# A four-layer graph network: the mixing products of three layers as 64x64 products in four quarters of the array

## What is computed

```python
# gnn, twice: W_left, W_right, W_lin per sublayer
u = u_left * adj_tri + u_left * diag_mask + u_right * swapaxes(adj_tri, 1, 2)
delta_exp_u = exp(u) * adj
attention = delta_exp_u / (sum(delta_exp_u, axis=2, keepdims=True) + 1e-10)
ctx = matmul(attention, h @ W_lin.T + b_lin)          # 64x64 times 64x384, per graph
h = relu(layer_norm(ctx) * ln_a + ln_b)

# gcn, twice: Wl, Ws, Wr per sublayer
attn = delta / (sum(delta, -1, keepdims=True) + 1e-10)   # delta = softmax(h h.T / temper) * adj
ctx = einsum(attn * upper, hl) + diag(attn)[..., None] * hs + einsum(attn * lower, hr)
h = relu(layer_norm(ctx) * g + beta)
```

## Time and profile before

| | |
|---|---|
| median of 3 runs | 3187.76 us (3184.48 to 3189.42) |
| the profiled execution: its time, its span | 3182.71 us, 3180.9 us |
| PE, DVE, ACT, POOL busy share of the span | 91%, 63%, 32%, 31% |
| granted TensorE clock, mean over the span | 0.968 of 2.4 GHz |
| steady period of a group: gnn first, gnn second | 25.99 us, 26.34 us |
| steady period of a group: gcn first, gcn second | 29.30 us, 29.13 us |

### The profile page before, as it was taken

How to read it: one execution, slowest core, us unless ns; L and a number is a source line. 1 busy time by engine, 2 the same in 40 slices (tenths; PEclk the granted TensorE clock), 3 DMA queues, 4 the chain that set the end, 5 groups by cost and what they waited for, 6 DMA issues and landing times.

```text
span 3180.9 us, 70089 instructions
## 1 busy us (share of the span) xinstructions
PE 2889.1 (91%) x25280; PEld 2445.8 (77%) x25280; DVE 2001.0 (63%) x4582; ACT 1014.4 (32%) x1921; POOL 974.3 (31%) x908
## 2 busy tenths in 40 slices
PE   6999979999959999997999997999996689899998
PEld 5888868888847777776888886888885577777776
DVE  4444434555556676666777775776776477777776
ACT  2333322333324444443222222122121333333432
POOL 1222213444433333332101110243334143334333
PEclk9999989999979999998999998999998899999999
DMA  3222242333311112112122114222222011111110
GB/s 97 70 69 69 59 129 77 99 99 99 96 61 45 45 45 66 45 52 88 44 64 64 54 43 126 64 75 94 94 75 89 31 45 45 45 35 33 45 35 33
DMA packets 197219, 210.27 MB, mean 66 GB/s; under 512 B 72736, under 2 KB 197024, under 8 KB 197024
## 3 DMA queue, kind: packets, MB, share of 16 engines
q1 hardware_dynamic: 197024, 207.33, 21.1%
HBM read 131.80 MB, written 75.50 MB: 65 GB/s over the span
## 4 chain that ended last, share of the span: by engine, by line
PE 52%; DVE 11%; issue 6%; ACT 1%; POOL 1%; DMA 1%; DVEq 0%; POOLq 0%; ACTq 0%
PE psum L1010 18%; PE psum L822 14%; PE psum L826 4%; DVE v_x L1419 3%; PE psum L1041 3%; PE psum L1040 3%; PE psum L851 2%; PE psum L840 2%; PE psum L895 2%; DVE room L1447 2%; PE psum L1022 2%; PE psum L872 1%; DVE room L1463 1%; DVE room L1377 1%; PE psum L863 1%
## 5 line engine op out<-in xcount | busy, mean ns | idle before, releaser
L1010 PE MATMUL psum<-fast 128*128 128x384 f32 x3456 | 647.8, 341 | 20.4 <-issue 8.1
L1010 PEld LDWEIGHTS psum<-fast 128*128 128x128 f32 x3456 | 596.2, 188 | 49.3 <-DVE room L1377 15.5
L1377 DVE TENSOR_TENSOR room<-psum,rows 128x384 f32<-128x384 f32 x512 | 283.9, 555 | 312.5 <-PE psum L1010 168.4
L822 PE MATMUL psum<-fast 128*128 128x512 f32 x1728 | 464.7, 416 | 3.8 <-DVE fast L1407 3.0
L694 PE MATMUL psum<-fast 128*128 128x512 f32 x1728 | 417.5, 398 | 16.2 <-DVE fast L1364 16.2
L694 PEld LDWEIGHTS psum<-fast 128*128 128x128 f32 x1728 | 327.0, 190 | 90.5 <-issue 16.9
L822 PEld LDWEIGHTS psum<-fast 128*128 128x128 f32 x1728 | 324.7, 196 | 75.5 <-issue 4.9
L540 POOL TENSOR_TENSOR room<-room 128x768 f32<-128x768 f32 x128 | 188.7, 1474 | 482.2 <-DVE room L1453 296.5
L826 PE MATMUL psum<-fast 128*128 128x384 f32 x1152 | 235.3, 348 | 42.8 <-DVE v_x L1419 30.1
L1211 ACT ACTIVATE room<-psum 128x512 f32<-128x512 f32 x192 | 114.6, 597 | 426.6 <-PE psum L694 426.6
L610 POOL TENSOR_TENSOR room<-room,halfs 128x4 f32<-128x4 f32 x32 | 33.3, 1042 | 704.8 <-DVE room L1699 704.8
(11 more groups left out here) (107 smaller groups left out, 4480.1 us busy)
## 6 DMA issues: line engine op xcount, KB each, us to landing
x_ring<-x_mid SPq DMA_DIRECT2D x64, 768.0 KB, 4.6
x_mid<-x_ring SPq DMA_DIRECT2D x48, 768.0 KB, 4.1
x_ring<-x_in SPq DMA_DIRECT2D x32, 768.0 KB, 4.6
z_mid<-x_ring SPq DMA_DIRECT2D x32, 768.0 KB, 4.1
z_sb<-z_mid SPq DMA_DIRECT2D x32, 768.0 KB, 5.9
adjc<-adj SPq DMA_DIRECT2D x96, 128.0 KB, 4.1
out<-x_ring SPq DMA_DIRECT2D x16, 768.0 KB, 4.1
w_raw<-w_all SPq DMA_DIRECT2D x19, 576.0 KB, 4.3
```

The lines of the kernel that those rows point to most:

```text
L822: mm = nc.tensor.matmul(dst, wpart[m][:, c, oc * P:(oc + 1) * P], hpart[G.par][:, c], start=(k == 0), stop=(k == 3 * C - 1))
L1010: mm = nc.tensor.matmul(dst[:, 0:H], hpart[G.par][:, c, t * P:(t + 1) * P], wpart[m][:, c, :], start=(k == 0), stop=(k == 3 * C - 1))
L1377: done(nc.vector.tensor_tensor(dst, src, rows[:, m], ALU.add), "evac_n")
```

## The change

- In gnn and gcn a mixing product is 64x64: one graph's matrix in one quarter of the array, 64 rows by 64 columns. The row half of a quarter is set by the partitions of the two operands, its column half by the partitions of the output. Two row halves that work at the same time write to different banks.
- gnn: `mix(g, pair)` issues four products, for a and b in (0, 1), with operands in row half b and output in column half a. For that the graphs of a group are taken in another order in stages 1 and 2: the turning writes its columns permuted, and the adjacency is read from two arrays that the host has permuted (`adj_q`, `adj_t`). `d_x` with its zeros becomes `d_k`, filled by one POOL operation of 128 partitions.
- gcn: the projection for the lower triangles is made with its rows shifted by one graph (`first_row`), so a graph's `hr` stands in the other partition half than its `hl`. The last tile wraps round to graph 0, for which ACT copies 64 columns behind the activations (`ninth_graph`, two operations for each group). Lower and upper products of different tiles then fill the four quarters: sixteen products in four rounds of four. Rounds 3 and 4 accumulate on rounds 1 and 2 and wait for them (`fs`). `d_x2` is half as large and filled by three DVE operations instead of four.
- Waits: the first gnn pair waits for `evac_n` 1 and the second for 3, before it was one for each tile; the gcn mixing waits at its start for `evac_n` 11, before for 8 to 11 in turn. DVE's `context` waits for a pair of tiles, and `gather` takes tiles 0, 2, 1, 3, the first two released after round 3 and the others after round 4.
- The memsets of the zeros are gone.

```diff
 # gnn, POOL
-                        for a in (0, 1):
-                            r = slice(a * S, (a + 1) * S)
-                            done(nc.gpsimd.tensor_tensor(d_x[r, :, r], et[r], biasc[r, g.par], ALU.mult), "dT")
+                        done(nc.gpsimd.tensor_tensor(d_k, et, biasc[:, g.par], ALU.mult), "dT")
 # gnn, TensorE
+                            turned = bank_of(g + 1, H_SLOT[c]).rearrange("p (i a b k) -> p i b a k", i=2, a=2, b=2)
                             for t in range(T):
-                                mm = nc.tensor.transpose(bank_of(g + 1, H_SLOT[c])[:, t * P:(t + 1) * P],
-                                                         z_sb[:, t, c * P:(c + 1) * P], ident)
+                                mm = nc.tensor.transpose(turned[:, t // 2, t % 2], z_sb[:, t, c * P:(c + 1) * P], ident)
...
-                    def mix(g, t):
-                        if t == 0:
-                            after(pe, "dT", g, 1)
-                        after(pe, "evac_n", g, t)
-                        after(pe, "z1", g + -1, t)
-                        done(nc.tensor.matmul(psum[:, 4 + t, 0:H + 1], d_x[:, t], lin[:, g.par, t], start=True, stop=True),
-                             "cx")
+                    def mix(g, pair):
+                        if pair == 0:
+                            after(pe, "dT", g, 0)
+                        after(pe, "evac_n", g, 2 * pair + 1)
+                        after(pe, "z1", g + -1, 2 * pair + 1)
+                        settle(pe)
+                        for a in (0, 1):
+                            for b in (0, 1):
+                                r, i = slice(b * S, (b + 1) * S), 2 * pair + a
+                                mm = nc.tensor.matmul(psum[a * S:(a + 1) * S, 4 + 2 * pair + b, 0:H + 1], d_k[r, i],
+                                                      lin[r, g.par, i], start=True, stop=True, skip_group_check=True)
+                        done(mm, "cx")
 # gcn, TensorE
+                        if j == 3 * T - 1:
+                            after(pe, "ninth", G, 0)
...
+                        first_row = t * P + (S if m == 2 else 0)
                         for c in range(C):
-                            for wpart, hpart in ((w_hi, h_hi2), (w_hi, h_lo2), (w_lo, h_hi2)):
-                                mm = nc.tensor.matmul(dst[:, 0:H], hpart[G.par][:, c, t * P:(t + 1) * P],
+                            for wpart, hpart in ((w_hi, h_hi9), (w_hi, h_lo9), (w_lo, h_hi9)):
+                                mm = nc.tensor.matmul(dst[:, 0:H], hpart[G.par][:, c, first_row:first_row + P],
...
-                        nc.tensor.matmul(psum[:, 4 + t, 0:H], d_x2[:, 0, t], lin3[:, g.par, 0, t], start=True, stop=False)
-                        done(nc.tensor.matmul(psum[:, 4 + t, 0:H], d_x2[:, 1, t], lin3[:, g.par, 2, t], start=False,
-                                              stop=True), "cx")
+                    def upper(g, t, a, first):
+                        r = slice(a * S, (a + 1) * S)
+                        return nc.tensor.matmul(psum[r, 4 + t, 0:H], d_x2[r, 0, t], lin3[r, g.par, 0, t], start=first,
+                                                stop=not first, skip_group_check=True)
+                    def lower(g, t, a, first):
+                        r = slice((1 - a) * S, (2 - a) * S)
+                        return nc.tensor.matmul(psum[a * S:(a + 1) * S, 4 + t, 0:H], d_x2[r, 1, t],
+                                                lin3[r, g.par, 2, (t - 1 + a) % T], start=first, stop=not first,
+                                                skip_group_check=True)
+                    def mix(g):
+                        after(pe, "dT", g, 2)
+                        after(pe, "evac_n", g, 3 * T - 1)
+                        after(pe, "cc", g + -1, T - 1)
+                        settle(pe)
+                        for t, u in ((0, 2), (1, 3)):
+                            upper(g, t, 0, True)
+                            upper(g, t, 1, True)
+                            lower(g, u, 0, True)
+                            done(lower(g, u, 1, True), "fs")
+                        for k, (t, u) in enumerate(((2, 0), (3, 1))):
+                            after(pe, "fs", g, k)
+                            settle(pe)
+                            upper(g, t, 0, False)
+                            upper(g, t, 1, False)
+                            lower(g, u, 0, False)
+                            done(lower(g, u, 1, False), "cx")
 # gcn, ACT: first in its body for g + 1
+                    def ninth_graph(G):
+                        after(act, "lo", G, C - 1)
+                        nc.scalar.activation(h_hi9[G.par][:, :, GT:], h_hi9[G.par][:, :, 0:S].bitcast(F32), ACT.Identity)
+                        done(nc.scalar.activation(h_lo9[G.par][:, :, GT:], h_lo9[G.par][:, :, 0:S].bitcast(F32),
+                                                  ACT.Identity), "ninth")
 # gcn, DVE
-                    def gather(g, t):
-                        after(dve, "cx", g, t)
+                    def gather(g, k):
+                        t = (0, 2, 1, 3)[k]
+                        after(dve, "cx", g, k // 2)
...
+                        if side == 0:
+                            done(nc.vector.tensor_tensor(d_x2[:, 0], d_T, mask[:, K_TRI, 0:S].unsqueeze(1).to_broadcast(
+                                [P, T, S]), ALU.mult), "dT")
+                            return
+                        for src, dst in ((top, low), (low, top)):
+                            done(nc.vector.tensor_tensor(d_x2[dst, 1], d_T[src], below[src], ALU.mult), "dT")
```

More of the change, by code:

```diff
@@ L267, in set_per @@
             if kind == "gnn":
[L268 removed]
+                st["aup"].per = st["cx"].per = 2
+            if kind == "gcn":
+                st["dT"].per, st["cx"].per, st["fs"].per = 3, 2, 2
             if kind.startswith("att"):
@@ L725, in body @@
                             part(g + 1, 0)
-                        for t in range(T):
-                            mix(g, t)
+                        mix(g, 0)
+                        mix(g, 1)
                         if one:
@@ L1046, in body @@
                             part(g + 1, 0)
-                        for t in range(T):
-                            mix(g, t)
+                        mix(g)
                         if one:
```

70 lines of the change are left out of this document (31 added, 39 removed), and 2 rows, old and new, of the table used.

## The result

The changed kernel takes 3105.77 us (median of 4 runs, 3103.01 to 3108.41), the kernel before beside it 3186.36 (4 runs, 3184.48 to 3189.42): a ratio of 0.9746, 95% interval 0.9729 to 0.9763. The forecast was 3136 with a range from 3108, so the kernel is 80.6 us faster where 51.7 were forecast, and it lies just outside the range. The sign and the gnn half were right; the gcn half was too small; and some 12 us came from a stage that the change doesn't touch.

A forecast was written before the change was run, and what follows sets the result against it. TensorE, 98 to 99% busy, was taken to bound gnn and gcn, with DVE taking back most of gcn's saving. Savings of 28.5 (gnn) + 23.2 (gcn) = 51.7 us from 3187.8 gave 3136 us, range 3108 to 3168.

The forecast's parts named there:

- Mixing on TensorE: Mixings in gnn and gcn: four quarters work at once, 1.29 us instead of 2.58 and 2.58 instead of 5.15.
- the slower rival: Mixing of all four stages: quarters don't go abreast, products start 0.322 us apart; 3255 us, chance 0.08.
- the way in: TensorE going from the whole array to tiles ahead of a mixing: 0.12 us.
- Switching: TensorE changing array mode and back around each mixing: costs 0.33 us, possibly 0.23 to 0.43.
- gnn: Both gnn stages: each group 0.95 us shorter, nothing else holding the period; 28.5 us in all.
- gcn: Both gcn stages: DVE takes back most of TensorE's 2.24 us; groups gain 0.61 and 1.04, 23.2 us in all.
- G: Start of the first gcn `gather`, counted from the mixing's start: second stage 1.49 us before, 2.27 after.
- Instruction supply: Rival in gcn's loop: TensorE stands still 2.9 us in each of 14 turns, 41 us on top; 3177 us, chance 0.03.
- the time between the stages: Ends of both gcn stages: the last gathers come 0.8 us later, giving 1.6 us back.
- everything arrives: Rival in gcn: all of TensorE's saving, 2.24 us a group, comes through despite DVE's gather; 3092 us, chance 0.06.

The follow-up runs named there:

- experiment 4: Changed kernel with each gnn mixing's products issued quarter by quarter and one semaphore for all eight: 3108.65 us.
- experiment 5: Changed kernel with part 1 of the next group issued between the two halves of the gnn mixing: 3111.40 us.
- experiment 3: Kernel before, with the first gcn gather waiting for the last mixed tile instead of the first: 3236.62 us.
- experiment 7: Changed kernel with DVE's gcn emptyings moved earlier: 3093.15 us; then also the second gcn stage's additions to x moved behind splits and emptyings: 3082.40 us.

## Why the prediction was right and wrong

**Mixing on TensorE: right.** Four abreast. The sixteen passes of gnn take 1.52 (1.3 + 0.16 forecast). The first gather comes at 2.33 (forecast 2.27), but that it is so near is in part luck: 0.12 of the 2.27 is the way in, which lies before the first record of the mixing, and the steps behind it took 0.18 more than reckoned. The case for the slower rival falls with experiment 4.

**Switching: right, a little low.** 0.33 forecast, 0.39 measured in experiment 5. The record of a mixing starts only once the way in is over, so a distance from that record leaves it out.

**gnn: right.** 0.95 a group forecast, 0.92 and 0.90 measured; the 0.06 of the switch is most of the difference. 28.5 us forecast, 27 measured. Here too DVE's operations were reckoned too slow: the four statistics end 3.0 us after the mixing's start (209.04 - 206.03) and not 3.3, but nothing waits for them.

**gcn: the mechanism right, one term mis-sized.** The gain is indeed cut by DVE's chain to `nat(3)`: TensorE waits ahead of parts 4 and 5, though not ahead of part 3 as forecast. The step that failed reads "DVE needs about 1.29 for each tile by itself, the two operations being 0.61 and 0.56 with a wait between them, so TensorE's rhythm of 1.29 and DVE's are the same by chance". An operation of 0.56 is followed by the next one 0.47 to 0.48 after its start, as the rows above show, and so the pace is 1.11 (experiment 3 measures it in the kernel before). In the second stage `nat(1)` started at G + 4.45 and ended at 4.99 where 5.64 was forecast; `nat(2)` started 1.62 behind `top_of` (1.75 forecast) and `nat(3)` 1.95 behind `nat(2)` (1.77). It ended at G + 9.04 where 9.66 was forecast, and part 5 starts at 11.52 and 11.72 in turn (its longer first record counted as in the prediction) where 12.09 was forecast, 0.47 earlier on average. The period gained 1.36 where 1.04 was, so 0.32 of that arrives: from part 5 to the next mixing the distance grew by 0.16, and most of this is the way in, 0.12, which the prediction had put at the front.

In the first stage the periods alternate between 28.26 and 27.45, gains of 1.04 and 1.85 where 0.61 was forecast. The faster gathers are in both. Most of the difference is that in every other group `nbb` takes 0.16 and not 0.70, so that `nat(3)` starts 2.27 behind `nat(2)` and not 2.84; this was not foreseen either, and why `nbb` alternates stays open. In sum 42 us came and 24.8 were forecast.

**Instruction supply: the rival was put to the wrong stage.** The gcn loops have no standstill, as thought. But att3, which already stood still at each turn's head, changed by some 12 us since its loop lies elsewhere in the program. The prediction put every stage that the diff doesn't touch at nothing, without a reason, and had no case for this. That is the second step that failed.

**Sum.** Of the 28 us by which the two profiled executions beat the forecast, 17 are gcn's, 13 att3's and 1 att1's; gnn takes 1 back and the time between the stages 2. It was forecast to grow by 1.6 and grew by 3.9 in this pair, but it differs by 3.5 between two executions of the kernel before, so that is no finding. Either miss alone, gcn's 17 or att3's 12, would have left the time inside the range. **Range:** it went two thirds of the way to "everything arrives" and nothing beyond. That rival was given 0.06, while experiment 7 shows that mostly DVE's order stood in its way.

## What to carry to other kernels

When an engine follows another at just the same pace, its own pace is not shown: take it from the nearest starts of the same operations where nothing holds them, or leave it open down to there. Lengths of records don't add up to it: an operation of 0.56 is followed after 0.47 or 0.48 here. When a hand-written order is tied to one engine's old speed, look at the other engine's list after a change: moving emptyings ahead and work that nobody waits for behind gave another 22 us here without touching TensorE. And where a loop stands still at each turn's head with nothing to wait for, an edit ahead of it in the program can change the untouched loop's time, here by 2%; tell this apart with some hundred idle instructions ahead of it.

## What the hardware showed beyond what was expected

Products of 64x64 issued quarter by quarter ran as fast as round the quarters (1.54 and 1.52 us for 16 passes). Whether loop turns of att3 have a second standstill, of up to 2.6 us, depends on the loop's place in the program, and it moved by 11 products when the loop moved by 24 instructions; with the heads' and the clock's share it is worth up to 16 us in a stage of 650. It ends 1.3 to 1.7 us after the landing of an instruction packet, the standstill at the head 1.6 to 1.8 after one. DVE's cast and subtraction on 128x512 take 0.42 and 0.69 us alone and up to 1.23 and 1.39 beside POOL's operations of 128x384.
